# A new order for four engines between a state-space scan and the first expert blocks, and a barrier replaced by single waits

## The reference, cut to what matters

```python
        dA = jnp.exp(A[None, None] * dt[..., None])
        dBx = dt[..., None] * B_ssm[:, :, None, :] * x_main[..., None]
        # h = dA_t * h + dBx_t ; y_t = sum over n of h * C_t   (the scan, 512 steps)
        y = y + x_main * D_param[None, None, :]
        y = y * jax.nn.silu(z)
        out = res_scale * (y @ out_proj_w) + residual
    ...
    x = x + L0_attn(_layernorm(x))
    h = _layernorm(x)
        gates = jax.nn.softmax(h @ router_w)          # 14 routed experts
        top_v, top_i = jax.lax.top_k(gates, 2)
        # each token: weighted sum of its 2 experts, plus 2 shared experts
    x = x + L0_ffn(h)
```

## Time and profile before

| what | value |
|---|---|
| runs, us | 1131.62, 1133.61, 1135.22; median 1133.61 |
| profiled execution: span from first to last instruction | 1232.4 us; no other time is given for this execution |
| mean granted TensorE clock in it | 0.851 |
| busy: PE, DVE, ACT, POOL | 74%, 69%, 63%, 58% of the span |
| end of the last scan instruction | 486.4 us |
| first matmul of the mixture | 615.1 us |
| last of the 64 sends issued | 634.3 us |
| first matmul of expert block 0 | 651.2 us |

### The profile page before, as it was taken

One profiled execution on the slowest core, in us unless ns is written; L12 is line 12 of the kernel. 1 busy time (PEld: TensorE's weight loads), 2 busy tenths in 40 slices (PEclk: granted clock), 3 DMA queues, 4 the chain that ended last, 5 costly groups with the idle time before them and its releaser, 6 DMA issues.

```text
span 1232.4 us, 15898 instructions
## 1 busy us (share of the span) xinstructions
PE 912.0 (74%) x4746; PEld 693.4 (56%) x4746; DVE 849.3 (69%) x1499; ACT 779.7 (63%) x1562; POOL 715.5 (58%) x536
## 2 busy tenths in 40 slices
PE   1995877877778788777279999734767649888882
PEld 1642665665656666666257777523545437666661
DVE  6755999999999998454356777443555457656646
ACT  1567888888788887332158888633555336666756
POOL 1221798999989997155573442664343560756660
PEclk9985899999999998776579999957777658988986
DMA  3002857667677673011135774211010124544306
GB/s 97 7 11 78 214 185 234 172 191 230 172 207 213 173 223 61 18 35 35 39 90 139 200 204 131 68 45 37 18 36 21 37 61 117 144 120 131 96 16 204
DMA packets 128023, 138.94 MB, mean 113 GB/s; under 512 B 16198, under 2 KB 86325, under 8 KB 127940
## 3 DMA queue, kind: packets, MB, share of 16 engines
q1 hardware_dynamic: 117820, 120.86, 35.4%
q0 software_dynamic: 9088, 16.94, 4.4%
q10 hardware_dynamic: 1032, 0.14, 0.1%
HBM read 76.60 MB, written 63.11 MB: 113 GB/s over the span
## 4 chain that ended last, share of the span: by engine, by line
PE 45%; DVE 15%; ACT 14%; issue 10%; another core or an unknown queue 7%; POOL 6%; DMA 2%; DVEq 0%; SPq 0%; ACTq 0%; POOLq 0%; PEldq 0%
PE ps L1661 8%; PE ps L1663 7%; PE ps L1662 7%; DVE arena L1285 7%; POOL arena L610 4%; PE ps L1755 3%; PE ps L1941 2%; ACT arena L831 2%; PE ps L1725 2%; PE ps L1900 2%; ACT arena L821 2%; PE ps L1763 2%; PE ps L2014 2%; PE ps L1822 1%
## 5 line engine op out<-in xcount | busy, mean ns | idle before, releaser
L610 POOL TENSOR_TENSOR arena<-arena 128x1024 f32<-128x1024 f32 x128 | 299.2, 2368 | 33.1 <-DVE arena L1285 31.8
L1285 DVE TENSOR_TENSOR_SCAN arena<-arena,ps 128x1024 f32<-128x1024 f32 x128 | 284.8, 2270 | 20.7 <-PE ps L1755 11.2
L635 POOL DMA_INDIRECT xs<-hx,slot x128 | 127.2, 994 | 138.0 <-DVE slot L1359 100.0
L1725 PE MATMUL ps<-ident,arena 128*128 128x128 f32 x1088 | 147.3, 285 | 17.7 <-POOL arena L610 14.9
L658 POOL DMA_INDIRECT yd<-yb,dest x92 | 99.5, 1081 | 84.7 <-ACT yb L938 55.6
L831 ACT ACTIVATE arena<-arena,bT 128x256 f32<-128x256 f32 x344 | 145.5, 494 | 0.0
L1725 PEld LDWEIGHTS ps<-ident,arena 128*128 128x128 f32 x1088 | 129.7, 148 | 25.6 <-POOL arena L610 20.9
L1755 PE MATMUL ps<-ident,arena 128*128 128x128 f32 x688 | 101.6, 295 | 52.6 <-DVE arena L1285 38.3
L1755 PEld LDWEIGHTS ps<-ident,arena 128*128 128x128 f32 x688 | 80.6, 150 | 95.2 <-ACT arena L831 78.1
L820 ACT ACTIVATE arena<-softplus_dt,Aneg 128x512 f32<-128x512 f32 x128 | 91.8, 717 | 39.0 <-DVE arena L1285 39.0
L1501 DVE TENSOR_TENSOR h_lo<-hs,h_hi 128x512 fp32r<-128x512 f32 x90 | 70.7, 800 | 49.8 <-ACT h_hi L917 47.2
(11 more groups left out here) (288 smaller groups left out, 2176.8 us busy)
## 6 DMA issues: line engine op xcount, KB each, us to landing
xs<-zero SPq DMA_DIRECT2D x16, 2340.0 KB, 11.1
arena<-bc_rows SPq DMA_DIRECT2D x64, 512.0 KB, 5.3
x_blk<-xs SPq DMA_DIRECT2D x52, 260.0 KB
w_raw<-in_L_ffn_w SPq DMA_DIRECT2D x58, 128.0 KB
ys<-yb SPq DMA_DIRECT2D x29, 256.0 KB, 2.5
big<-yd SPq DMA_DIRECT2D x8, 512.0 KB, 4.7
w_raw<-in_L_ffn_Wg SPq DMA_DIRECT2D x23, 128.0 KB
w_raw<-in_L_ffn_Wu SPq DMA_DIRECT2D x23, 128.0 KB
```

What stands on the lines that cost most here:

```text
L610: nc.gpsimd.tensor_tensor(hc[M % 3], h[N % 3], row.unsqueeze(1).to_broadcast([P, NG, L]), ALU.mult)\
L635: pool.indirect_dma_start(out=xs, out_offset=bass.IndirectOffsetOnAxis(ap=slot[:, q, t:t + 1], axis=0), in_=hx[:, t, :], in_offset=None).t ...
L1285: nc.vector.tensor_tensor_scan(h[N % 3].rearrange("p g t -> p (g t)"), dA[N % 2].rearrange("p g t -> p (g t)"), ps[N % 2][:, :, :].rearran ...
L1725: return nc.tensor.matmul(out_, in_, ident[:, :], is_transpose=True, start=first_, stop=False, skip_group_check=True)
```

## The change

Barrier 4 is taken out. SP and POOL, which waited for it, wait for the last scan instead; PE waits in `project_y(0)` until DVE has copied y of the last batch out of `ps[2]`; the wait for the constant tables moves into `count_group` (and so is also met in layer 1, 8 times). On DVE, that copy (`take_y(7)`) now stands between `gate_y(0)` and `gate_y(1)`. The loops over G on PE, ACT and DVE are replaced by written-out lists of the same steps. The functions, their operands and their buffers are the same. POOL's and SP's programs keep their order.

```diff
-        BARRIERS = (1, 3, 4, 7, 8, 11)
+        BARRIERS = (1, 3, 7, 8, 11)
...
-            sp.wait_ge(phase_done, ended(4))
+            sp.wait_ge(sc["scan"], NM)
...
-            pool.wait_ge(phase_done, ended(4))
+            pool.wait_ge(sc["scan"], NM)
...
-            barrier(act, 4)
-
-            for G in range(NGRS[0] + 1):
+            copy_gated(0)
+            silu_z(2)
+            copy_gated(1)
+            copy_gated(2)
+            silu_z(3)
+            silu_z(4)
+            copy_gated(3)
+
+            scale_rows(0)
+            scale_rows(1)
+            silu_z(5)
+            take_routed(0)
+            take_routed(1)
+            copy_gated(4)
...
-            for b in range(2):
-                gate_y(b)
+            gate_y(0)
             take_y(NB - 1)
-            barrier(dve, 4)
-
+            gate_y(1)
...
+            gate_y(2)
+            add_o(0)
+            add_o(1)
+            gate_y(3)
+            scales(0)
+
+            add_o(2)
+            gate_y(4)
+            add_o(3)
+            scales(1)
+            gate_y(5)
+            pick_group(0, 0)
+
+            add_o(4)
+            place_group(0, 0)
+            gate_y(6)
+            add_o(5)
+            scales(2)
+            pick_group(0, 1)
+            gate_y(7)
+            place_group(0, 1)
+
+            add_o(6)
+            pick_group(0, 2)
+            add_o(7)
+            scales(3)
+            place_group(0, 2)
+
+            pick_group(0, 3)
+            place_group(0, 3)
...
             def project_y(b):
                 pe.wait_ge(po["gc"], b + 1)
+                if b == 0:
+                    pe.wait_ge(sc["y"], NB)
...
             def count_group(k, G):
                 E, GT = EXPERTS[k], GTS[k]
+                pe.wait_ge(consts, TABLES)
...
+            channel_major(0)
+            project_z(2)
+            channel_major(1)
+            project_y(0)
+            channel_major(2)
+            project_y(1)
+            project_z(3)
+            project_y(2)
+            project_z(4)
+            channel_major(3)
+            project_z(5)
+            project_y(3)
+            channel_major(4)
+
+            columns_of(0)
+            columns_of(1)
+            logits_of(0)
+            logits_of(1)
+            project_y(4)
+
+            columns_of(2)
+            count_group(0, 0)
+            channel_major(5)
+            project_z(6)
+            project_y(5)
...
+            columns_of(6)
+            columns_of(7)
+            logits_of(6)
+            logits_of(7)
+            count_group(0, 3)
             count_all(0)
```

More of the change, by code:

```diff
@@ L867, in _ @@
                 silu_z(b)
-            barrier(act, 4)
-            for G in range(NGRS[0] + 1):
[L871 to L881, removed]
+            copy_gated(0)
[11 more added lines that the diff above has]
+            copy_gated(4)
+            scale_rows(2)
+            scale_rows(3)
+            copy_gated(5)
+            silu_z(6)
+            take_routed(2)
+            take_routed(3)
+            scale_rows(4)
+            silu_z(7)
+            scale_rows(5)
+            copy_gated(6)
+            take_routed(4)
+            take_routed(5)
+            copy_gated(7)
+            scale_rows(6)
+            scale_rows(7)
+            take_routed(6)
+            take_routed(7)
             def moe(k):
@@ L1803, in _ @@
             output_sum(item(NM - 1) - 1)
-            barrier(pe, 4)
             def channel_major(b):
@@ L1866, in _ @@
                 .then_inc(made_pe, 1)
[L1867 to L1887, removed]
+            channel_major(0)
[21 more added lines that the diff above has]
+            project_y(5)
+            columns_of(3)
+            logits_of(2)
+            logits_of(3)
+            project_z(7)
+            channel_major(6)
+            columns_of(4)
+            count_group(0, 1)
+            columns_of(5)
+            project_y(6)
+            channel_major(7)
+            logits_of(4)
+            logits_of(5)
+            project_y(7)
+            count_group(0, 2)
+            columns_of(6)
[3 more added lines that the diff above has]
+            count_group(0, 3)
             count_all(0)
```

## The result

The kernel with the change takes 1128.99 us (median of 20 runs, 1127.62 to 1132.51), the kernel before, run beside it on the same chip, 1132.69 us (20 runs, 1128.76 to 1135.22). The ratio is 0.9971 with a 95% interval of 0.9962 to 0.9980: faster by 3.3 us by the ratio (3.7 by the two medians), where 10 were forecast; the time lies inside the range.

A forecast was written before the change was run, and what follows sets the result against it. The routing stage was taken as bound by hand-overs between engines, the expert blocks by PE. Block 0 was to start 6.8 to 27 us earlier, 10 taken: 1133.6 - 10 = 1124 us, range 1107 to 1133.

The forecast's parts named there:

- What the runs will keep of it: Whole kernel: the profiled execution is 98.8 us longer than the median; gain between 6.8 and 27 us, 10 taken.
- the stalls: Routing stage: four stretches without work under sends in flight, 20.4 us in all, possibly missing from the runs.
- The barrier: Start of the routing stage: taking it out frees PE by 2 to 2.7 us; moved table wait costs at most 0.4.
- The first send: POOL's first send: added PE work fills idle time, moving it by +0.6 to +5.3 us; +2 taken, so 531.
- The other sends: POOL's 64 sends: three gaps, 22.8 us, go; sends end at 614 instead of 634.3, 20 us earlier.
- Block 0: First expert block: PE about 2 us early, waits for the load; start at 624 instead of 651.2, 27 us less.
- Rules against it: POOL's sends: DVE instructions with two SBUF operands hold them up, costing 1 to 3 us.
- Rival 4: POOL's sends: 16 low_h of 0.80 us hold them up, 13 us in full; 1140 us; chance 0.04.
- The second: Rival: gain spent before the sends, first send 5 us late, lower clock at block 0; 1131 to 1134; chance 0.22.
- The first: Rival: the profile's stalls are in the runs too; gain 20 to 27 us, 1107 to 1113; chance 0.16.
- third: Rival: first addresses too late, first send at 545, block 0 7 us slower; 1141 us; chance 0.08.

The follow-up runs named there:

- e1: The kernel before, unchanged, profiled once more: 1132.3 us, span 1130.6 us.
- e2: The kernel before with barrier 4 taken out and the loops over G kept: 1123.13 us, ratio to before 0.9932.
- e3: The kernel before with the written-out lists and the barrier kept: ratio to before 1.0006.
- e5: The change, no barrier, with lists that put group 0's steps ahead of later batches' work: 1124.77 us, ratio to before 0.9935.
- e7: The change with 32 of layer 0's 64 row sends left out: ratio to before 0.9788.
- e8: The kernel before with 32 of layer 0's 64 row sends left out: ratio to before 0.9995.
- e9: e5 with 20 transpositions of the identity on PE between project_y(2) and columns_of(0), filling a wait: ratio to before 0.9923.
- e6: The kernel before, barrier kept, with 18 transpositions of the identity filling PE's wait at it: ratio to before 1.0000.
- e10: e2 with 12 transpositions of the identity filling PE's wait in project_y(0): ratio to before 0.9911.

## Why the prediction was wrong, point by point

- **What the runs will keep of it: the step that failed.** The prediction had seen that the stalls may be missing in the runs, and set the ends at 6.8 and 27 us. The step that failed is the choice of 10 between them: it kept a part of the profile's stalls for the kernel before in its runs, because "the excess of 98.8 has to be somewhere". The runs had none of it, and 76.0 of the 101.8 us lay behind block 0 (1232.4 - 651.17 against 1130.6 - 625.41), where by the prediction "all is as before". Even the low end was too high: without the stalls block 0 of the kernel before was put at 630.8 us, and e1 has it at 625.41. Only idle time that nothing explained (20.4 us) had been taken off. 25.8 us went, since work had been slowed along with it: the logits at 568.37 took 3.43 us in the profile shown, in e1 the same ones, at 563.91, 1.85; and the clock from the first send to the shared experts was 0.63, in e1 0.75 (526 to 594 us). What block 0 gained was 3.2 us (625.4 less after's 622.25), 4.6 counted from the gate, and 3.3 are measured. That the time lies in the range says little for the mechanism: the range is 26 us wide and was drawn to hold both values of the stalls.
- **The barrier: mis-sized.** Its gain was put at 2 to 2.7 us of waiting. The wait was 2.69 us, but e2 gained 7.7 (5.5 to 9.8), and PE's work in the stage ran at a higher clock in it. The prediction used both levels of `project_y` as prices of added work and never asked what the barrier's removal does to the level. The wait for the tables cost nothing that can be seen: layer 1's first four counts start 0.75 to 0.78 us behind the start of the matmuls before them, in e1 and after alike.
- **The first send.** Moved by +0.6 to +5.3, +2 taken, so 531. It came at 526.75. With the barrier in, the list costs 0.9 us (e3); without it 3.8 us (after against e2), inside the range, and at the higher clock. (The range's high end had `project_z` at 1.9 us, its time at the higher level; at the lower one it took 3.32 us in e5.) Counted from the gate the first send came 3.1 us earlier than in e1, and that is most of the 4.4 us by which the sends end earlier; 2.3 are the one gap, and 1.0 goes to the row's longer sends.
- **The other sends.** An unbroken row of 83 us was right, 84.8 measured. But the gaps that it was to close were 2.29 us in the clean kernel, not 22.8.
- **Block 0.** PE was put 2 us too early at the transposition; it was 17.02 us too early. The addresses of the last group came at 569.92, not at 583, and PE was through with the shared experts' part ahead of the transposition in 26.3 us, not 31.8 (26.6 in e1). So nearly all that the order gains (23.6 us of PE's path, e7 against e8) falls into PE's wait.
- **Rules against it.** Sends were held up little. All over-long sends of after together cost 65.6 - 64 x 0.96 = 4.2 us (e1: 3.5). Rival 4, each `low_h` adding its whole length, did not come: 12 `low_h` lay under sends in after, and the sends beside them took 1.1 us more than 0.96 each in all. But DVE does hold sends up, and by a fixed pattern. DVE and POOL in after, timelines: two instructions with two SBUF operands, and the sends that began under them.

```profile
577.84 1.09 DVE L1478 TENSOR_TENSOR tail<-tail,late 128x896 f32<-128x896 f32 x1
577.92 1.83 POOL L635 DMA_INDIRECT xs<-hx,slot  x1 [0.31 <-issue]
...
590.80 0.69 DVE L1537 TENSOR_TENSOR h_lo<-hs,h_hi 128x512 fp32r<-128x512 f32 x1 [0.28 <-ACT h_hi L937]
590.93 1.40 POOL L635 DMA_INDIRECT xs<-hx,slot  x1 [0.31 <-issue]
```

  Both sends end 0.82 and 0.84 us behind the end of the DVE instruction. So does, within 0.82 to 0.84 us, each of the other sends of after that took over 1.05 us, apart from the very first (1.21 us). A send of 0.96 us that begins under such an instruction is thus held only for what is left of it, and not at all where less than some 0.13 us are left (0.96 - 0.83), which is why a whole `low_h` is seldom added. Beside `x<-x,ps` (one operand in PSUM, at 597.72) the send took 0.96 us. The Trainium skill, "SBUF — State Buffer", section "Who interferes with whom", says that such a VectorE instruction contends with a GpSimd instruction that reads SBUF, under an exclusive lock, and that the order of issue decides which of the two waits; these sends agree.
- **Rivals.** The second is what happened, in its main sentence: the path of the sends bounds all that the order could give, and block 0 starts at the lower clock (5.85 us from transposition to first matmul where e1 has 4.28). It had put 0 to 3 us as left; 3.3 are (2.3 to 4.3). Its reason for the loss, a first send 5 us later, was not it: the 6.8 us were not there to lose. The first, third and fourth are out: no stalls in the runs, no first send behind 538, no hold-up of the sends in the size of 13 us.

## What to carry to other kernels

Look at how long the profiled execution is against the runs before pricing anything in it: where it is 9% longer, take a second one. Taking out the idle time that nothing explains is not enough: that was 20.4 of the 25.8 us here. Where two paths meet (here PE's and the sends'), compute both on both sides of the change; relieving one by 23.6 us is worth only what the other has to spare, and then the work that this frees room for is worth moving: on e9 one constant, five shared batches first in place of four, brought 11.3 us, over three times the whole change. And a list that fills every wait is not the best list: what starts the long serial row, here the first send, has to go first.

## What the runs showed of the hardware

- One profiled execution had stalls that the runs and the next profile of the same kernel don't have: 1232.4 against 1130.6 us, with gaps of 5.45, 9.54 and 7.82 us on POOL where e1 has 2.29 us and none. What caused them stays open.
- Taking out a barrier at which PE waited 2.69 us gained 7.7 us (5.5 to 9.8, e2). PE's wait at the barrier did not set the clock's level of the whole stage by itself: e6 removed the wait's idle time and lost as much PE work to the lower clock as before (25.3 and 24.7 us), e2 removed the barrier and lost 11.7. Why the loops keep the higher level in e2 and e10 and not in e6 was not settled; the three differ also in when DVE, ACT and POOL reach their work.
- A send that POOL issued while DVE ran a TENSOR_TENSOR on two SBUF operands ended 0.82 to 0.84 us behind that instruction's end, up to 1.83 us long instead of 0.96 (after; the sends over 1.05 us in the other runs show the same, the first send of a run aside).
- The end of the scan moved by up to 5 us between profiles, more than the change is worth, so single traces were compared only from a common event on. Whether it moves with the execution or with the program was not separated.
